# First cross attention: keys' projection and the last key's product in strips of 32 columns

## The chip, the cores and the metric

The kernel runs on one core of a Trainium2 chip. The metric is device time in microseconds; three runs of the kernel before took 3436.03 to 3438.41 us, with a median of 3437.31. All arithmetic around the change is in FP32. TensorE runs an FP32 matmul as two passes: every matmul of the code stands in the trace as two MATMULs and two LDWEIGHTS.

## What is computed

Six blocks act on `x` (128 x 32 x 256): a cross attention, a differential attention and a feed-forward block, then another three of the kind. The change touches the first block alone, which is, cut to what matters:

```python
x = x + xattn(layernorm(x), ctx)          # ctx: 128 batches x 257 keys x 256
q = rms_norm(linear(xn, q_w, q_b))        # 16 heads of 16
k = rms_norm(linear(ctx, k_img_w, k_img_b))
v = linear(ctx, v_img_w, v_img_b)
out = linear(softmax(q @ k.T * scale) @ v, o_w, o_b)
```

## The kernel before

The first cross attention (`image_attention`) goes through 128 slots, one per batch, in a software pipeline; four slots are one chunk of 128 tokens. `every_slot` writes out the first and the last slots and runs those between in a loop (`Fori`, line 137) whose body holds four. Each engine has its own program, in the order in which the code stands, and the engines wait for one another by semaphores. 257 keys are 256, which go through TensorE in two halves of 128, and a last one, whose terms are worked out apart.

TensorE's slot, function `tensor`, in this order:

- L366, the keys' projection for the batch two slots on: the context, transposed, is the weights (128 rows, 128 columns), `w_k` streams with 256 columns. Two halves of the keys times two of the contraction are 4 matmuls, 8 passes. Its end raises `k_full`, for which VectorE's L698 (`k_raw`) waits. It writes the PSUM bank `a_ps`.
- L376, four transposes of the scaled keys of the next batch. It waits for `turn_read[1]` of ScalarE and `k_scaled` of GpSimd.
- L381, the values' projection of the next batch, in the same form as L366. Its end raises `v_full`, behind which SyncE issues the load of a later context.
- an item of the chunk, one in each of four slots: output projection (L390), a transpose (L394), the queries (L398), a transpose (L405).
- L414 and L418, four transposes each, of this batch's weights of attention.
- L429, the scores of the next batch, as tiles of 32 rows and 64 columns.
- L442, the weighing: attention's weights times values, as 16 matmuls with 32 columns of weights each (tiles of 128 rows and 32 columns), the four in a row going to the four groups of 32 PSUM partitions of `out_ps`.
- L448, in every fourth slot: the last key's product for the chunk, two matmuls of 128 columns, into the other half of the same bank (`item_ps`). It waits for `v_last_ready` of GpSimd and for `p_rows_ready`, which VectorE raises at L746.

Then follows L366 of the next slot. The wait ahead of L366 is for `turn_read[0]` and for the context's load. In the trace, `128*32` in a row is the tile of the array: rows, columns. The second cross attention (`adapter_attention`) has a similar slot, with L976 for the scores (tiles of 32 rows and 128 columns), L980 for transposes and L1091 for the weighing (tiles of 128 rows and 32 columns).

Of the kernel before, what the change touches and what calls it, by code (L numbers as in the profile page):

```python
# [14 lines left out]
P = 128  # L15
D = 256
# [70 lines left out]
def ge(eng, sem, count):  # L87

    if not isinstance(count, int) or count > 0:
        eng.wait_ge(sem, count)  # L90
# [91 lines left out]
def image_attention(nc, io, stack):  # L182
# [16 lines left out]
    def sb(name, shape, dt=F32):  # L199
        return stack.enter_context(nc.sbuf_tensor(f"{name}_i", shape, dt))  # L200

    def pb(name):
        return stack.enter_context(nc.psum_tensor(f"{name}_i", [P, 512], F32))
# [9 lines left out]
    w_q, w_k, w_v, w_o = (sb(n, [P, 2, D]) for n in ("w_q", "w_k", "w_v", "w_o"))  # L213
# [7 lines left out]
    ctx_t = [sb(f"ctx_t{j}", [P, 2, 2 * P]) for j in range(4)]  # L221
# [8 lines left out]
    v_last_all, v_last_raw, v_last = sb("v_last_all", [P, D]), sb("v_last_raw", [P, D]), sb("v_last", [P, D])  # L230
# [6 lines left out]
    p_last, p_last_t, p_rows = sb("p_last", [P, L]), sb("p_last_t", [P, L]), sb("p_rows", [P, 4, L])  # L237
# [6 lines left out]
    q, q2, qn = sb("q", [P, D]), sb("q2", [P, D]), sb("qn", [P, D])  # L244
# [4 lines left out]
    a_ps, b_ps, c_ps, out_ps = pb("a_ps"), pb("b_ps"), pb("c_ps"), pb("out_ps")  # L249
    out_heads = out_ps[:, 0:P].rearrange("p (f h q) -> p f h q", f=2, h=2)  # L250
    item_ps, nf_sum_ps = out_ps[:, 2 * P:4 * P], out_ps[:, P:P + 3]
# [39 lines left out]
    def item_out(at):  # L291

        b = at.b()
        if b == 0:
            return y_ready, at.chunks(-1)
        return (None, xn_t_ready, q_raw, q_t_ready)[b], at.chunks(1)

    def has_item(at):
        return at.live_chunk(-1) if at.b() == 0 else at.live_chunk(1)
# [56 lines left out]
    def tensor(pe, before, ahead):  # L356
        def slot(at):
            if at.live(2):
                if at.live(-1):
                    pe.wait_ge(turn_read[0], at.count(-1))  # L360
                else:
                    ge(pe, k_raw_ready, at.count(1))
                pe.wait_ge(ctx_in[at.b(2)], at.chunk(2) * 16 + 16)
                for r in range(2):
                    for c in range(2):
                        last = pe.matmul(a_ps[:, r * D:r * D + D], ctx_t[at.b(2)][:, c, r * P:r * P + P], w_k[:, c, :], start=c == 0, stop=c == 1)  # L366
                last.then_inc(k_full, 1)
            if at.live(1):
                if at.live(-1):
                    pe.wait_ge(turn_read[1], at.count(-1))  # L370
                else:
                    ge(pe, k_ready, at.count(0))
                pe.wait_ge(k_scaled, at.count(1, 2))
                for f in range(2):
                    for r in range(2):
                        last = pe.transpose(b_ps[:, f * D + r * P:f * D + r * P + P], k_raw[at.b(1) % 2][:, r, f * P:f * P + P], ident)  # L376
                last.then_inc(k_turned, 1)
                ge(pe, v_ready, at.count(0))
                for r in range(2):
                    for c in range(2):  # L380
                        last = pe.matmul(c_ps[:, r * D:r * D + D], ctx_t[at.b(1)][:, c, r * P:r * P + P], w_v[:, c, :], start=c == 0, stop=c == 1)  # L381
                last.then_inc(v_full, 1)
            if has_item(at):
                if at.live(-1):
                    pe.wait_ge(out_read, at.count(-1))
                elif has_item(At(at.i, at.o - 1)):
                    ge(pe, *item_out(At(at.i, at.o - 1)))
                if at.b() == 0:
                    for f in range(2):
                        last = pe.matmul(item_ps, attn_t[:, f, :], w_o[:, f, :], start=f == 0, stop=f == 1)  # L390
                elif at.b() == 1:
                    pe.wait_ge(xn_ready, at.chunks(1))
                    for c in range(2):
                        last = pe.transpose(item_ps[:, c * P:c * P + P], xn[:, c * P:c * P + P], ident)  # L394
                elif at.b() == 2:
                    pe.wait_ge(xn_t_ready, at.chunks(1))
                    for c in range(2):
                        last = pe.matmul(item_ps, xn_t[:, c, :], w_q[:, c, :], start=c == 0, stop=c == 1)  # L398
                    if isinstance(at.i, int) and at.n() == NF_SUM:
                        pe.wait_ge(nf_total_ready, 1)  # L400
                        last = pe.matmul(nf_sum_ps[0:S, :], nf_ones[:, :], nf_total[:, :], start=True, stop=True)
                else:
                    pe.wait_ge(qn_ready, at.chunks(1))
                    for c in range(2):
                        last = pe.transpose(item_ps[:, c * P:c * P + P], qn[:, c * P:c * P + P], ident)  # L405
                last.then_inc(item_full[at.b()], 1)
            if isinstance(at.i, int) and at.n() == B - 1:
                for _ in range(8):
                    pe.matmul(b_ps[:, 0:D], w_k[:, 0, 0:P], w_k[:, 1, :], start=True, stop=True)
            if at.live():  # L410
                ge(pe, k_raw_ready, at.count(2))
                pe.wait_ge(probs_ready, at.count(0, T))
                for i in range(T):
                    last = pe.transpose(a_ps[:, i * P:i * P + P], probs[:, i, 0:P], ident)  # L414
                last.then_inc(turned[0], 1)
                ge(pe, k_ready, at.count(1))
                for i in range(T):
                    last = pe.transpose(b_ps[:, i * P:i * P + P], probs[:, i, P:2 * P], ident)  # L418
                last.then_inc(turned[1], 1)
            if at.live(1):  # L420
                pe.wait_ge(k_ready, at.count(1))
                pe.wait_ge(k_last_ready, at.count(1))
                pe.wait_ge(q_bd_ready, at.count(1))
                if not at.live():
                    pe.wait_ge(first_out, 3)
                for f in range(2):
                    for i in range(T):
                        rows = slice(32 * i, 32 * i + 32)
                        last = pe.matmul(s_ps[i][64 * f:64 * f + 64, 0:K], q_bd[at.b(1) % 2][rows, f, :, :].rearrange("p h q -> p (h q)"), k_n[rows, f, :], start=True, stop=True)  # L429
                        if f == 1:  # L430
                            last.then_inc(scores_done, 1)
            if at.live():
                if has_item(at):
                    ge(pe, *item_out(at))
                else:
                    ge(pe, out_read, at.count(-1))
                ge(pe, v_ready, at.count(0))
                for r in range(2):
                    pe.wait_ge(turn_read[r], at.count(0))
                    for f in range(2):  # L440
                        for g in range(4):
                            last = pe.matmul(out_ps[32 * g:32 * g + 32, f * 64:f * 64 + 64], v[at.b() % 2][:, r, f * P + 32 * g:f * P + 32 * g + 32],  # L442
                                             probs_t[r][:, g * P + f * 64:g * P + f * 64 + 64], start=r == 0 and f == 0, stop=r == 1, skip_group_check=True)
                if at.b() == 3:
                    pe.wait_ge(v_last_ready, at.chunks(0))
                    pe.wait_ge(p_rows_ready, at.chunks(0))
                    for f in range(2):
                        last = pe.matmul(item_ps[:, f * P:f * P + P], v_last[:, f * P:f * P + P], p_rows[:, :, :].rearrange("p b q -> p (b q)"),  # L448
                                         start=False, stop=True, skip_group_check=True)
                last.then_inc(out_done, 1)  # L450

        pe.wait_ge(const_ready, 1)
# [3 lines left out]
        for f in range(2):  # L456
            for c in range(2):
                last = pe.matmul(s_ps[0][:, f * P:f * P + P], w_k[:, c, f * P:f * P + P], ctx_last[:, c, :], start=c == 0, stop=c == 1)
        last.then_inc(first_full, 1)
        pe.wait_ge(const_in, 16)  # L460
        slot(At(-1, 0))
        slot(At(-1, 1))
        pe.wait_ge(first_ss_ms, 1)
# [3 lines left out]
        for c in range(2):  # L467
            last = pe.matmul(s_ps[2][:, 0:D], ctx_last[:, c, :], w_v[:, c, :], start=c == 0, stop=c == 1)
# [4 lines left out]
        for f in range(2):  # L473
            last = pe.matmul(s_ps[3][:, 0:D], v_b[:, f:f + 1].broadcast_to([P, P]), w_o[:, f, :], start=f == 0, stop=f == 1)
# [2331 lines left out]
```

## Time and profile before

| | |
|---|---|
| median of three runs | 3437.31 us |
| profiled execution | 3437.49 us, span 3435.6 us |
| first cross attention | about 12 to 916 us |
| PE, DVE, ACT, POOL busy in the span | 98%, 71%, 57%, 48% |
| PE busy between 12 and 916 us | 890 of 904 us |

PE is TensorE's matmul, PEld its loading of weights, DVE VectorE, ACT ScalarE, POOL GpSimd, SP SyncE. Passes of TensorE overlap, and their ends are modelled: the time that one pass takes of the engine is the distance from its start to the next one's start. A row of the timeline merges passes of one line; its first column is the start of the first, its second the distance from there to the end of the last.

### The profile page before, as it was taken

The numbers are of one execution on the slowest core, as the hardware profiler recorded it, in microseconds if no ns is written. First come the engines' busy times: TensorE is split into PE (matmuls) and PEld (weight loads), VectorE is DVE, ScalarE is ACT, GpSimd is POOL, SyncE is SP. The second block draws the span as 40 slices with busy tenths as digits, with TensorE's granted clock in tenths as the row PEclk, the third lists the DMA queues.
The fourth block names the chain that finished last, engine by engine and source line by source line (L and its number), as shares of the span: only waits on it lengthen the run. The fifth ranks groups of instructions, "written<-read, shape, count | busy, mean of one in ns | idle before, by whom it ended". The sixth has DMA issues, their size and how long they took to land.

```text
span 3435.6 us, 92591 instructions
## 1 busy us (share of the span) xinstructions
PE 3361.4 (98%) x29689; PEld 2484.9 (72%) x29698; DVE 2446.6 (71%) x7409; ACT 1960.2 (57%) x5935; POOL 1647.2 (48%) x3197
## 2 busy tenths in 40 slices
PE   9999999999899999999999999999999999999999
PEld 7888888888666767777777777777766666665555
DVE  5677877777787648888888888888868844444443
ACT  5777777777566537777776777776765411111111
POOL 4666666666565536655665565566546400000000
PEclk9999999999999999999999999999999999999999
DMA  3111111111212231111111111111135620000000
GB/s 96 57 54 53 56 53 53 55 53 56 65 51 70 81 109 44 45 46 42 44 46 42 48 46 41 45 46 42 47 79 145 184 64 20 20 19 20 19 19 9
DMA packets 280323, 187.59 MB, mean 55 GB/s; under 512 B 117165, under 2 KB 277125, under 8 KB 280213
## 3 DMA queue, kind: packets, MB, share of 16 engines
q1 hardware_dynamic: 279925, 185.75, 19.0%
q8 instruction: 66, 1.08, 0.1%
q10 hardware_dynamic: 288, 0.40, 0.1%
q14 instruction: 44, 0.36, 0.0%
HBM read 145.61 MB, written 36.21 MB: 53 GB/s over the span
## 4 chain that ended last, share of the span: by engine, by line
PE 51%; DVE 7%; issue 2%; ACT 2%; DMA 1%; SPq 0%; DVEq 0%; ACTq 0%; POOL 0%; POOLq 0%
PE bank_e L2551 13%; PE bank_e L2528 6%; PE a_ps_a L1011 5%; PE b_ps_a L969 5%; PE s_ps_a L976 4%; PE a_ps_a L980 3%; PE out_ps_a L1091 3%; PE c_ps_a L980 2%; PE b_ps_a L1023 2%; DVE neg_max_a L1203 2%; ACT probs_a L1112 1%; PE out_ps_a L1078 1%; PE m_ps_r L2146 1%; PE b_ps_a L1018 1%; PE b_ps_a L1036 1%
## 5 line engine op out<-in xcount | busy, mean ns | idle before, releaser
L1112 ACT ACTIVATE probs_a<-s_ps_a,neg_max_a 128x257 f32<-128x257 f32 x1024 | 472.2, 476 | 283.5 <-DVE neg_max_a L1203 283.5
L1154 POOL TENSOR_SCALAR probs_a<-probs_a,gated_a 128x256 f32<-128x256 f32 x1024 | 495.2, 503 | 269.3 <-DVE gated_a L1211 269.3
L1203 DVE TENSOR_REDUCE neg_max_a<-s_ps_a 128x1 f32<-128x257 f32 x1024 | 360.9, 414 | 0.0
L2577 ACT ACTIVATE gate_e<-bank_e 128x512 f32<-128x512 f32 x128 | 76.4, 597 | 493.1 <-PE bank_e L2551 493.0
L523 POOL TENSOR_SCALAR probs_i<-probs_i,inv_sum_i 128x256 f32<-128x256 f32 x512 | 244.8, 492 | 127.9 <-DVE inv_sum_i L687 123.4
L2694 DVE TENSOR_TENSOR hidden_e<-gate_e,bank_e 128x512 f32<-128x512 f32 x128 | 87.3, 687 | 292.5 <-PE bank_e L2551 290.9
L2509 POOL TENSOR_TENSOR inv_std_e<-var_eps_e,half_e 128x4 f32<-128x4 f32 x8 | 8.1, 1010 | 567.2 <-DVE var_eps_e L2591 567.2
L507 ACT ACTIVATE probs_i<-s_ps_i,neg_max_i 128x257 f32<-128x257 f32 x512 | 236.3, 474 | 69.7 <-DVE neg_max_i L758 68.0
L366 PE MATMUL a_ps_i<-w_k_i,ctx_t_i 128*128 128x256 f32 x1024 | 253.6, 391 | 5.5 <-issue 5.5
L1011 PE MATMUL a_ps_a<-w_v_a,ctx_t_a 128*128 128x256 f32 x1024 | 256.7, 394 | 0.0
L381 PE MATMUL c_ps_i<-w_v_i,ctx_t_i 128*128 128x256 f32 x1024 | 242.2, 379 | 0.0
L2551 PE MATMUL bank_e<-xn_t_e,w_gate_e 128*128 128x512 f32 x512 | 241.3, 593 | 0.0
L969 PE MATMUL b_ps_a<-ctx_t_a,w_qk_a 128*128 128x256 f32 x1016 | 240.4, 379 | 0.4 <-issue 0.4
L2551 PE MATMUL bank_e<-xn_t_e,w_up_e 128*128 128x512 f32 x512 | 240.6, 592 | 0.0
L1011 PEld LDWEIGHTS a_ps_a<-w_v_a,ctx_t_a 128*128 128x128 f32 x1024 | 184.8, 190 | 69.8 <-issue 25.5
L2528 PEld LDWEIGHTS bank_e<-w_down_e,hidden_e 128*128 128x128 f32 x1024 | 194.6, 190 | 50.3 <-issue 26.8
L2528 PE MATMUL bank_e<-w_down_e,hidden_e 128*128 128x256 f32 x1024 | 230.1, 379 | 0.0
L366 PEld LDWEIGHTS a_ps_i<-w_k_i,ctx_t_i 128*128 128x128 f32 x1024 | 185.4, 191 | 36.7 <-issue 10.4
L758 DVE TENSOR_REDUCE neg_max_i<-s_ps_i 128x1 f32<-128x257 f32 x512 | 181.3, 415 | 41.2 <-PE s_ps_i L429 41.1
L1112 ACT ACTIVATION_READ_ACCUMULATOR probs_a<-s_ps_a,neg_max_a 128x1 f32 x1024 | 210.4, 205 | 0.0
L976 PE MATMUL s_ps_a<-k_t_a,q_bd_a 32*128 32x289 f32 x2048 | 197.0, 454 | 11.9 <-ACT probs_a L1112 6.7
L381 PEld LDWEIGHTS c_ps_i<-w_v_i,ctx_t_i 128*128 128x128 f32 x1024 | 184.6, 190 | 19.8
(365 smaller groups left out, 8059.7 us busy)
## 6 DMA issues: line engine op xcount, KB each, us to landing
ctx_t_i<-in_ctx_t SPq DMA_DIRECT2D x128, 256.0 KB, 2.7
ctx_t_a<-in_ctx_t SPq DMA_DIRECT2D x128, 256.0 KB, 2.7
mask_a<-in_L_xattn_mask SPq DMA_DIRECT2D x512, 4.0 KB, 1.5
v_bd_a<-v_self_a SPq DMA_DIRECT2D x512, 8.0 KB, 1.8
x_tok_i<-in_x SPq DMA_DIRECT2D x32, 128.0 KB, 2.0
x_res_i<-in_x SPq DMA_DIRECT2D x32, 128.0 KB, 2.4
x_after<-y_tok_i SPq DMA_DIRECT2D x32, 128.0 KB, 1.7
x_tok_d<-x_after SPq DMA_DIRECT2D x32, 128.0 KB, 2.2
```

The costliest lines, as they stand in the source:

```text
L366: last = pe.matmul(a_ps[:, r * D:r * D + D], ctx_t[at.b(2)][:, c, r * P:r * P + P], w_k[:, c, :], start=c == 0, stop=c == 1)
L381: last = pe.matmul(c_ps[:, r * D:r * D + D], ctx_t[at.b(1)][:, c, r * P:r * P + P], w_v[:, c, :], start=c == 0, stop=c == 1)
L507: act.activation(probs[:, i, :], s_ps[i][:, 0:K], ACT.Exp, bias=neg_max[:, i:i + 1], accum_out=row_sum[:, i:i + 1]).then_inc(exp_done, 1)
L523: pool.tensor_scalar(probs[:, i, 0:2 * P], probs[:, i, 0:2 * P], inv_sum[:, i:i + 1], 1.0, ALU.mult, ALU.mult).then_inc(probs_ready, 1)
L969: last = pe.matmul(into[:, f * n:f * n + n], w_qk[:, c, D + f * P:D + f * P + P], ctx[:, c, 0:n], start=c == 0, stop=c == 1)
L976: pe.matmul(s_ps[:, g, 0:N], q_bd[j][rows, f, :, :].rearrange("p h q -> p (h q)"), k_t[j][rows, f, :], start=True, stop=True).then_inc(sco ...
L1011: last = pe.matmul(a_ps[:, r * D:r * D + D], ctx_t[at.b(1)][:, c, r * P:r * P + P], w_v[:, c, :], start=c == 0, stop=c == 1)
L1112: act.activation(probs[:, t, :], s_ps[:, g, 0:K], ACT.Exp, bias=neg_max[:, t:t + 1], accum_out=row_sum[:, t:t + 1]).then_inc(exp_done, 1)
L1154: pool.tensor_scalar(probs[:, t, 0:2 * P], probs[:, t, 0:2 * P], gated[:, t:t + 1], 1.0, ALU.mult, ALU.mult).then_inc(probs_ready, 1)
L1203: dve.tensor_reduce(neg_max[:, 4 * f + g:4 * f + g + 1], s_ps[:, g, 0:K], AX.X, ALU.max, negate=True).then_inc(max_ready, 1)
L2528: last = pe.matmul(w[:, t * D:t * D + D], hidden[e % 2][:, k, tok:tok + P], w_down[:, e, k, :], start=k == 0, stop=k == TILES - 1)
L2551: last = pe.matmul(w[:, :], weights[:, e, c, t * P:t * P + P], xn_t[:, c, :], start=c == 0, stop=c == 1)
```

## The change

The four matmuls of L366 become sixteen: each takes 32 columns of the context as weights and writes 32 PSUM partitions. The two of L448 become eight in the same way. Operands, sums, waits, semaphores and the order of the lines stay as they are.

```diff
-                        last = pe.matmul(a_ps[:, r * D:r * D + D], ctx_t[at.b(2)][:, c, r * P:r * P + P], w_k[:, c, :], start=c == 0, stop=c == 1)
+                        for g in range(4):
+                            last = pe.matmul(a_ps[32 * g:32 * g + 32, r * D:r * D + D], ctx_t[at.b(2)][:, c, r * P + 32 * g:r * P + 32 * g + 32], w_k[:, c, :],
+                                             start=c == 0, stop=c == 1, skip_group_check=True)
...
-                        last = pe.matmul(item_ps[:, f * P:f * P + P], v_last[:, f * P:f * P + P], p_rows[:, :, :].rearrange("p b q -> p (b q)"),
-                                         start=False, stop=True, skip_group_check=True)
+                        for g in range(4):
+                            last = pe.matmul(item_ps[32 * g:32 * g + 32, f * P:f * P + P], v_last[:, f * P + 32 * g:f * P + 32 * g + 32], p_rows[:, :, :].rearrange("p b q -> p (b q)"),
+                                             start=False, stop=True, skip_group_check=True)
```

## Rows read from the trace of the kernel before

**Rows 1.** The page: busy time, chain that ended last, shortest DMA to land.

```profile
PE 3361.4 (98%) x29689; PEld 2484.9 (72%) x29698; DVE 2446.6 (71%) x7409; ACT 1960.2 (57%) x5935; POOL 1647.2 (48%) x3197
...
PE 51%; DVE 7%; issue 2%; ACT 2%; DMA 1%; SPq 0%; DVEq 0%; ACTq 0%; POOL 0%; POOLq 0%
...
mask_a<-in_L_xattn_mask SPq DMA_DIRECT2D x512, 4.0 KB, 1.5
```

**Rows 2.** Busy time by stretch: us, each engine, granted clock, DMA share, GB/s.

```profile
12.00:916.00 904.00, 890.14 (x10264) 726.57 (x10264) 677.09 (x2108) 661.96 (x2143) 579.39 (x1153) 1.00 0.19 57
```

**Rows 3.** TensorE's waits, 12 to 916 us: total us, times, longest us.

```profile
PE a_ps_i L366 <- issue: 5.5, 29, 0.2
...
PE b_ps_i L376 <- POOL k_raw_i L543: 1.1, 1, 1.1
```

**Rows 4.** Timeline of TensorE: start us, us, instruction.

```profile
407.37 0.65 PE L442 MATMUL out_ps_i<-probs_t_i,v_i 128*32 128x64 f32 x32
...
410.22 1.89 PE L381 MATMUL c_ps_i<-w_v_i,ctx_t_i 128*128 128x256 f32 x8
```

**Rows 5.** Timeline of TensorE around L366 in an ordinary slot, partly in narrow windows.

```profile
407.80 0.22 PE L442 MATMUL out_ps_i<-probs_t_i,v_i 128*32 128x64 f32 x1
...
407.95 1.99 PE L366 MATMUL a_ps_i<-w_k_i,ctx_t_i 128*128 128x256 f32 x8
...
408.27 0.38 PE L366 MATMUL a_ps_i<-w_k_i,ctx_t_i 128*128 128x256 f32 x1
...
409.78 0.60 PE L376 MATMUL b_ps_i<-const_i,k_raw_i 128*128 128x128 f32 x4
```

**Rows 6.** Timeline of TensorE in the second cross attention, partly in narrow windows.

```profile
1503.37 0.42 PE L976 MATMUL s_ps_a<-k_t_a,q_bd_a 32*128 32x289 f32 x4
1503.72 0.33 PE L980 MATMUL a_ps_a<-const_a,probs_a 128*128 128x128 f32 x1
...
1503.88 0.38 PE L980 MATMUL a_ps_a<-const_a,probs_a 128*128 128x128 f32 x2
...
1507.35 1.08 PE L1091 MATMUL out_ps_a<-probs_t_a,v_a 128*32 128x128 f32 x32
```

**Rows 7.** Timeline of TensorE behind the loop's branch, partly in narrow windows.

```profile
421.87 0.22 PE L442 MATMUL out_ps_i<-probs_t_i,v_i 128*32 128x64 f32 x1
...
422.29 1.99 PE L366 MATMUL a_ps_i<-w_k_i,ctx_t_i 128*128 128x256 f32 x8 [0.20 <-issue]
424.11 0.60 PE L376 MATMUL b_ps_i<-const_i,k_raw_i 128*128 128x128 f32 x4
```

**Rows 8.** Line 137, 100 to 850 us: ns min/median/max, first and last start.

```profile
L137 PEldq COMPARE_BRANCH  x27: 215/215/220, 115.9 to 838.6; - x27
```

**Rows 9.** Busy time by stretch: one pass of either cross attention's loop.

```profile
394.16:421.95 27.79, 27.48 (x328) 22.52 (x320) 22.17 (x68) 20.69 (x67) 18.25 (x37) 1.00 0.18 54
1378.22:1417.94 39.72, 39.45 (x375) 30.70 (x370) 34.44 (x112) 28.11 (x92) 23.77 (x54) 1.00 0.17 45
```

**Rows 10.** Timeline of TensorE and VectorE around L448, partly in narrow windows.

```profile
414.13 0.29 DVE L746 TENSOR_TENSOR p_rows_i<-p_last_t_i,const_i 128x128 f32<-128x128 f32 x1
...
414.31 0.24 PE L442 MATMUL out_ps_i<-probs_t_i,v_i 128*32 128x64 f32 x4
414.57 0.68 PE L448 MATMUL out_ps_i<-p_rows_i,v_last_i 128*128 128x128 f32 x4
...
416.82 0.38 PE L376 MATMUL b_ps_i<-const_i,k_raw_i 128*128 128x128 f32 x2
```

**Rows 11.** Line 448: idle time of its engine before it, us and times.

```profile
  issue: 3.5, 22
```

**Rows 12.** The same as group 10 in a later slot.

```profile
691.43 0.29 DVE L746 TENSOR_TENSOR p_rows_i<-p_last_t_i,const_i 128x128 f32<-128x128 f32 x1
...
692.40 0.23 PE L442 MATMUL out_ps_i<-probs_t_i,v_i 128*32 128x64 f32 x2
...
694.84 0.27 PE L376 MATMUL b_ps_i<-const_i,k_raw_i 128*128 128x128 f32 x1
```

## Prediction

> **What bounds the kernel now.** I read the page first, for the share of each engine, then the busy time by stage, the waits of TensorE in the stage that the diff touches, the timeline of a few of its slots, and last narrow windows of that timeline, since the question is one of tenths of a microsecond. The page has TensorE busy for 98% of the span and on half of the chain that ended last [rows 1]. The first cross attention is the stretch from 12 to 916 us: TensorE is busy for 890 of 904 us there, at a granted clock of 1.00, which is the 2.4 GHz level [rows 2]. In the whole stretch it waits for another engine's work for some 8 us, and the only wait of its own that comes back regularly is 29 times 0.2 us at L366 [rows 3]. So this stage lasts as long as TensorE's own stream, and all that lies between the starts of its passes counts: what the diff saves or adds there moves the end by as much. "Busy" hides such losses, because the modelled end of a pass lies behind the start of the next one; starts have to be compared.
>
> **What a change of tiling costs.** A pass of 256 columns through the whole array starts 0.216 us behind the one before it (8 passes of L381 in 1.89 us, the last alone 0.38, so 7 steps in 1.51) [rows 4]. The weighing (L442) runs in strips: its 32 passes in four column groups take 0.65 us, 0.22 of them the last pass alone, so 0.43 between first and last start: 7 steps from one group of four to the next of 0.056 us, 0.02 for the four starts within a group, and 0.02 more once, for the first, short weight loads [rows 4]. Now the boundary to the keys' projection (L366): the last strip starts at 407.80, the projection at 407.95, its second pass only at 408.27 [rows 5]. Without a change of tiling the next pass would start 0.056 - 0.02 = 0.04 us behind the last strip. It starts 0.15 behind it, which is 0.11 lost; the second pass comes 0.32 instead of 0.216 later, since the first weights were not loaded ahead: 0.10 lost. From the last strip to the first turn of keys (L376, 409.78) it is 1.98 us. Between the projection and L376 nothing is lost (the last pass starts 0.38 before the end of the group at 409.94, so at 409.57, and L376 0.216 later) [rows 5], since both use the whole array.
>
> **What the change does: it moves that boundary, it does not remove it.** The projection becomes 16 matmuls with 32 columns of weights instead of 4 with 128, so 32 passes instead of 8, in 8 groups of four; multiplications, bytes and waits are the same. The turns behind it (L376) still use the whole array, and so the tiling changes between L366 and L376 now. No row shows strips followed by L376. The nearest ones are in the second cross attention: behind the 32-row strips of L976 (289 columns, 0.24 us of streaming at the rate above) the transpose L980 starts 0.33 us after the last strip (1503.39 to 1503.72), and its second pass 0.16 later instead of 0.11 [rows 6]. So a drain of 0.09 behind the end of the stream and 0.055 for the uncovered weights [rows 6], which is half of the 0.10 at L366. That half is all that the change has to win.
>
> That four strips of a projection run side by side at full speed is the second thing without a row. The nearest is L1091, strips of the same shape with 128 columns: 32 passes in 1.08 us less 0.27 for the last, 0.81 = 7 x 0.109 + 0.02 + 0.025, and 0.109 is the step of whole-array passes of 128 columns too (four of L376 from 409.78 to L381 at 410.22) [rows 4 to 6]. I take 0.216 for 256 columns. Its bounds: nothing lost, or the first group's 0.025 lost again in each group.
>
> **The Trainium skill**, in TensorEngine Tiling, Key Properties, says that changing the tiling mode drains the engine, not merely changing the tile. The 0.15 at L442 to L366 agrees [rows 5]; by that rule the count of changes decides, and it stays three in a slot. The same page, under Restrictions, says that column tiling rules out the FP32 transpose mode; no run here shows it. By that the turns could not follow in strips, and the drain has to come back in front of them.
>
> **The sum, by kind of slot,** each from the last strip of the weighing to L376.
> Ordinary (62 slots, two in four): 1.98 now. After: 0.04, then 7 x 0.216 = 1.51 to the last group, 0.02 to its last strip, 0.213 of streaming and 0.096 of drain, and 0.055 of uncovered weights: 1.935. Minus 0.045 each, -2.8 us.
> Behind the loop's branch (29 slots, those of L366's waits [rows 3]): TensorE's sequencer branches for 0.215 us [rows 8], and the projection starts 0.42 us behind the last strip (421.87 to 422.29), with L376 at 424.11: 2.24 us [rows 7]. The drain in front of L366 costs nothing here, as it lies under the branch. After: 0.42 + 0.025 + 1.51 + 0.02 + 0.31 + 0.055 = 2.34. Plus 0.10 each, +2.8 us.
> Slots with the last key's product (31, one in four). In 23 of them, up to 667 us, L448 waits for `p_rows` (22 such waits are long enough to be listed [rows 11]): VectorE ends it at 414.42, L448 starts at 414.57, the last strip had started at 414.33; L376 follows at 416.82, 2.49 us [rows 10]. The wait covers the drain here too, and it stays: `p_rows` hangs on VectorE's order behind L405 of this same slot, and from L405 to L442 nothing changes. After: 0.24, 0.025 and 4 groups x 0.109 for L448, then 1.51 + 0.02 + 0.31 + 0.055 = 2.60. Plus 0.11 each, +2.5 us. In the other 8, once VectorE has left the quantizer's steps behind, `p_rows` is ready long before (691.72): 2.43 now (692.41 to 694.84) [rows 12], after 0.04 + 0.44 + 1.895 = 2.375; -0.4 us.
> The first two projections have no strips ahead of them, so they pay a change of tiling on both sides: +0.3 us.
> Together +2.4 us: the half of a weight load that is won in two slots of four is lost where a branch or a wait had been covering the drain.
>
> Two terms with a bound. TensorE's sequencer must have issued the strips in time: it issues the 64 instructions of the weighing between two of its own steps, in under 0.6 us, and stands just a few loads ahead at the boundary. If it comes late by up to 0.05 us there, 70 slots cost up to 3.5 us more; I take 0, as L442 itself keeps a step of 0.056 per four strips, a quarter of the 0.216 that is needed here [rows 4]. If the transposes' weights should be loaded during the drain, 124 x 0.055 = 6.8 us less; I take 0.055, by L980. `k_full` comes 0.2 us earlier against the turns in ordinary slots; VectorE's L698 needs it, but no wait of TensorE hangs on it. L376 waits for `k_scaled` of POOL, and only once for 1.1 us; coming 0.1 earlier, it finds it ready [rows 3]. SP's loads of the context are issued behind `v_full`, which moves by 0.1 us at most and lies three slots ahead of its use.
>
> The profiled execution took 3437.49 us for a span of 3435.6; the median of the runs is 3437.31, so they are alike, and I predict 3437.31 + 2.4 = 3439.7 us.
>
> **The rivals.**
> The change does not do what it says: the drain in front of L366 stays, because what drains is not the tiling but any change of shape. Then the ordinary slots pay both sides, 62 x 0.13 = 8 us more, some 3448. Against it: L366 to L376 changes line, operands and columns without loss as long as the tiling is the same [rows 5]. Chance 4%.
> The whole boundary goes: the turns behind strips start without drain or load. Ordinary slots then win 1.98 - 1.77 = 0.21 (13 us), slots behind the branch and with a wait 0.07 (3.6 us), the other 8 0.23 (1.8 us): 3419. For it speaks that the stretch from L442 to L366 is now one stream. Against it is L980 behind L976 [rows 6]. Chance 6%. A half-way case, the drain stays but the load is hidden, gives 3437.31 + 2.4 - 6.8 = 3433. Chance 12%.
> Slower: strips of 256 columns do not keep the pace of 0.216, because four weight loads and four streams of moving columns, all reading the same `w_k`, come at once. There are 128 x 8 = 1024 groups, so from 0.007 us per group on (3%) it is a measurable loss; with the 0.025 of a first group in every one of the other seven it is 22 us, 3462. For it: no strip with more than 128 columns is in the trace. Against it: L1091 is exact at 128. Chance 9%.
> Slower as well: the loop's body on TensorE grows from 648 instructions by 4 x 48 + 24 to 864, above the 745 of the second cross attention [rows 9]. Were the branch to wait for instructions from memory, at no less than the 1.5 us in which the shortest transfer lands [rows 1], 27 to 29 passes of the loop would add 43 us: 3483. For it: no body so large is in the trace. Against it: the branches of the loop that is there take 0.215 us, with the wait behind them as short as 0.2 [rows 8, 3]. Chance 4%. The Trainium skill (Runtime: NRT & Kernel Launch, Instruction fetch mechanics) gives TensorE room for 2048 instructions; by that page nothing is fetched again.
>
> **How the numbers follow.** The forecast itself, with its bounds, has 65%: from 3433 (load hidden) to 3443.5 (sequencer late), and a microsecond for the spread of the medians. With the half-way case it is 77%; the range 3431.5 to 3445.0 takes in these and a small part of the slower rivals. A measurement of this kernel can tell 0.2%, 6.9 us, from no change: faster is below 3430.4, slower above 3444.2. Faster 0.08, same 0.76, slower 0.16.
>
> **What the profile of the changed kernel will show.** L366 as 4096 passes of 128*32, first one 0.04 us behind the last strip of L442 in ordinary slots, 0.42 behind a branch; its groups of four 0.216 apart, L376 0.31 behind the last strip and its second pass 0.16 later. L448 as 512 passes, still starting 0.24 behind L442 up to 667 us. Slots of one kind as long as before within 0.1 us. I am wrong if the groups are further apart, if the branch takes more than 0.22, or if L376 starts less than 0.3 behind the last strip.

## The result, and the profile after

The changed kernel takes 3441.07 us (median of 20 runs, 3435.96 to 3445.16), the kernel before 3435.11 (20 runs, 3433.04 to 3438.41): a ratio of 1.0016, 95% interval 1.0009 to 1.0022. That is some 6 us more, and less than the 0.2% taken as the bound of "no change". The profiled execution has a span of 3438.9 us, 3.3 more than before.

The first cross attention first. Timeline of TensorE in the changed kernel (start us, us, instruction), partly in narrow windows; L444 is the weighing, L367 the keys' projection, L378 the turns of the keys, L383 the values' projection, L451 the last key's product:

```profile
406.50 0.65 PE L444 MATMUL out_ps_i<-probs_t_i,v_i 128*32 128x64 f32 x32
406.97 1.91 PE L367 MATMUL a_ps_i<-w_k_i,ctx_t_i 128*32 128x256 f32 x32
408.81 0.66 PE L378 MATMUL b_ps_i<-const_i,k_raw_i 128*128 128x128 f32 x4
409.30 1.89 PE L383 MATMUL c_ps_i<-w_v_i,ctx_t_i 128*128 128x256 f32 x8
...
408.50 0.38 PE L367 MATMUL a_ps_i<-w_k_i,ctx_t_i 128*32 128x256 f32 x1
...
413.40 0.22 PE L444 MATMUL out_ps_i<-probs_t_i,v_i 128*32 128x64 f32 x1
...
413.65 0.65 PE L451 MATMUL out_ps_i<-p_rows_i,v_last_i 128*32 128x128 f32 x16
414.08 1.94 PE L367 MATMUL a_ps_i<-w_k_i,ctx_t_i 128*32 128x256 f32 x32
415.95 0.33 PE L378 MATMUL b_ps_i<-const_i,k_raw_i 128*128 128x128 f32 x1
...
421.04 0.24 PE L444 MATMUL out_ps_i<-probs_t_i,v_i 128*32 128x64 f32 x4
421.47 1.93 PE L367 MATMUL a_ps_i<-w_k_i,ctx_t_i 128*32 128x256 f32 x32 [0.19 <-issue]
423.34 0.66 PE L378 MATMUL b_ps_i<-const_i,k_raw_i 128*128 128x128 f32 x4
```

Against [rows 5]: the last strip of the weighing starts at 406.93 (406.50 + 0.65 - 0.22), the first of the projection 0.04 later instead of 0.15, and then nothing is lost within the projection: last strip at 408.50, so 7 x 0.216 + 0.02 behind the first. The turns start 0.31 behind that last strip, and the values' projection follows 0.49 us behind the turns' start instead of 0.44 (0.055 of uncovered weights). In all 1.88 us from strip to turns, 1.93 with the weights, against 1.98 in this slot; over the 65 ordinary slots it is 0.041 us less on average. Against [rows 10]: L451 starts 0.25 behind the last strip, as before; the turns 2.55 behind it instead of 2.49, plus 0.055. Against [rows 7]: 0.41 and 2.28, plus 0.055, instead of 0.42 and 2.24. Over all slots that is, from the first to the last pass of the values' projection (start of the first, start of the last, on the right):

```profile
L381 PE MATMUL c_ps_i<-w_v_i,ctx_t_i x1024: 379/379/382, 22.1 to 905.6; 128*128 128x256 f32 x171
```

in the kernel before, 883.5 us, and in the changed one

```profile
L383 PE MATMUL c_ps_i<-w_v_i,ctx_t_i x1024: 379/379/382, 19.8 to 905.2; 128*128 128x256 f32 x171
```

885.4 us: **1.9 us more**, where 2.4 was forecast. (The changed kernel came to its first pass 2.3 us earlier: the granted clock between 11 and 18 us was 1.00 in that execution and 0.51 in the one before. That is outside the change, and a second execution of it began at 21.8. Between the first and the last pass of the values' projection the clock was at its upper level throughout, in every profile of this study.)

**The other loss is far from the change**, in the fifth block (self attention of the second three), from its first transposes to the first transposes of the sixth. Kernel before, then after:

```profile
2554.60 1.09 PE L2133 MATMUL m_ps_r<-const_r,xn_r 128*128 128x128 f32 x8
2746.76 1.35 PE L2536 MATMUL bank_e<-ident_e,xn_e 128*128 128x128 f32 x8
```

```profile
2554.20 1.09 PE L2136 MATMUL m_ps_r<-const_r,xn_r 128*128 128x128 f32 x8
2749.89 1.35 PE L2539 MATMUL bank_e<-ident_e,xn_e 128*128 128x128 f32 x8
```

192.2 us against 195.7: **3.5 us more** in a block whose code is the same. In the stretch between the two cross attentions (last pass of the values' projection to the first of L969, at 1273.74 us and 1273.32) the kernels take 368.2 and 368.1 us, from there to the fifth block both take 1280.9, and behind the fifth block 688.8 and 689.0. In the fifth block, what first meets the eye is a wait for transfers. TensorE's waits between 2550 and 2760 us, before and after:

```profile
PE s_ps_r L2154 <- DMA by_dim_q_r<-scratch_q: 2.4, 3, 1.5
```

```profile
PE s_ps_r L2157 <- DMA by_dim_q_r<-scratch_q: 6.2, 6, 2.1
```

These two lines alone prove little. The kernel before has another 3.3 us at the same line, put down to ScalarE, and TensorE is idle for 17.4 us of the block before and 17.6 after. It is busy for 3.3 us more after (178.1 against 174.7), and its clock was at the lower level for 13.7 us of the block instead of 6.8. So the clock is a rival; it is taken up behind the experiments.

The block writes keys and queries to memory and reads them back in another order; SyncE issues the reading once the writing has landed. One such pair in the fourth turn, before and after, by the times of issue (the writing, then the reading):

```profile
2629.45 0.56 SPq L2036 DMA_DIRECT2D scratch_q<-proj_t_q_r  x1
2633.64 1.34 SPq L2041 DMA_DIRECT2D by_dim_q_r<-scratch_q  x2
```

```profile
2629.60 0.61 SPq L2039 DMA_DIRECT2D scratch_q<-proj_t_q_r  x1
2635.03 1.34 SPq L2044 DMA_DIRECT2D by_dim_q_r<-scratch_q  x2
```

And DMA between the issue of the writing and that of the reading (queues with packets, MB and share; then the issue with its time to landing).

```profile
q1 hardware_dynamic: 2254, 0.76, 93.4%
issues: line engine op xcount, KB each, median us to landing
scratch_q<-proj_t_q_r SPq DMA_DIRECT2D x1, 256.0 KB, 4.2
```

```profile
q1 hardware_dynamic: 2222, 0.75, 68.1%
q8 instruction: 1, 0.02, 1.4%
issues: line engine op xcount, KB each, median us to landing
scratch_q<-proj_t_q_r SPq DMA_DIRECT2D x1, 256.0 KB, 5.4
```

```profile
q8 instruction: 66, 1.08, 0.1%
```

```profile
q8 instruction: 69, 1.13, 0.1%
```

and the growth of TensorE's program fits the three: a written-out projection has 48 more instructions and there are 12 of them (8 outside the loop, 4 in it), a last key's product 24 more in 3 places: 648 instructions, 2.5 packets of 256. Hence a theory for the fifth block: it is written out, its instructions are streamed in while it runs (20 packets of queue 8 in the kernel before), and by the change each packet is fetched at another point of a turn, the 648 leaving a remainder of 136 when divided by the 256 that a packet holds. The rival was that strips, or the clock, or chance made the difference. The experiments bear on both parts, the first cross attention and the fifth block.

### The profile page after: what moved, and what is told of

Read it like the earlier page. It is cut to its first block, busy times and chain, and to the rows that moved or that the text cites. A ratio compares the mean times of both kernels' runs of the same rounds, so it can differ in the third digit from the quotient of the medians.

```text
span 3438.9 us, 99512 instructions
## 1 busy us (share of the span) xinstructions
PE 3365.5 (98%) x33154; PEld 2413.9 (70%) x33154; DVE 2448.5 (71%) x7409; ACT 1960.4 (57%) x5935; POOL 1648.4 (48%) x3197
## 4 chain that ended last, share of the span: by engine, by line
PE 50%; DVE 7%; DMA 2%; issue 2%; ACT 1%; SPq 0%; DVEq 0%; ACTq 0%; POOL 0%; POOLq 0%
PE bank_e L2554 13%; PE bank_e L2531 6%; PE a_ps_a L1014 5%; PE b_ps_a L972 5%; PE s_ps_a L979 4%; PE a_ps_a L983 3%; PE out_ps_a L1094 3%; PE c_ps_a L983 2%; PE b_ps_a L1026 2%; DVE neg_max_a L1206 2%; ACT probs_a L1115 1%; PE out_ps_a L1081 1%; PE m_ps_r L2149 1%; DMA scratch_q<-proj_t_q_r 1%; DMA by_dim_q_r<-scratch_q 1%
## 5 line engine op out<-in xcount | busy, mean ns | idle before, releaser
L367 PE MATMUL a_ps_i<-w_k_i,ctx_t_i 128*32 128x256 f32 x4096 | 246.0, 380 | 5.2 <-issue 5.2
L383 PE MATMUL c_ps_i<-w_v_i,ctx_t_i 128*128 128x256 f32 x1024 | 242.2, 379 | 0.0
L972 PE MATMUL b_ps_a<-ctx_t_a,w_qk_a 128*128 128x256 f32 x1016 | 240.4, 379 | 0.4 <-issue 0.4
L383 PEld LDWEIGHTS c_ps_i<-w_v_i,ctx_t_i 128*128 128x128 f32 x1024 | 184.6, 190 | 19.8
L972 PEld LDWEIGHTS b_ps_a<-ctx_t_a,w_qk_a 128*128 128x128 f32 x1016 | 183.1, 190 | 20.5 <-DVE v_self_a L1252 0.9
```

The lines of the kernel that those rows point to most:

```text
L367: last = pe.matmul(a_ps[32 * g:32 * g + 32, r * D:r * D + D], ctx_t[at.b(2)][:, c, r * P + 32 * g:r * P + 32 * g + 32], w_k[:, c, :], star ...
L972: last = pe.matmul(into[:, f * n:f * n + n], w_qk[:, c, D + f * P:D + f * P + P], ctx[:, c, 0:n], start=c == 0, stop=c == 1)
```

## The experiments

All lengths in one table, each from one profiled execution: A is the first cross attention (first to last pass of the values' projection), B the fifth block, "place" the instructions added to TensorE ahead of the fifth block, modulo 256. "Low clock" is the time within B for which TensorE's clock was granted at its lower level, "delayed" how many of the block's eight writings of queries were delayed, which is explained behind the experiments.

| kernel | place | A, us | B, us | low clock, us | delayed | ratio to before, 95% interval |
|---|---|---|---|---|---|---|
| before | 0 | 883.5 | 192.2 | 6.8 | 0 | |
| before again | 0 | 883.5 | 192.6 | 10.2 | 0 | 0.9999 (0.9990 to 1.0008) |
| changed | 136 | 885.4 | 195.7 | 13.7 | 4 | 1.0016 (1.0009 to 1.0022) |
| changed again | 136 | 885.5 | 196.0 | 13.7 | 4 | 1.0018 (1.0009 to 1.0027) |
| strips in L366 alone | 64 | 891.8 | 199.1 | 10.2 | 4 | 1.0037 (1.0025 to 1.0049) |
| strips in L448 alone | 72 | 886.7 | 196.9 | 13.7 | 3 | 1.0027 (1.0017 to 1.0038) |
| before, 136 instructions more | 136 | 883.4 | 195.9 | 10.2 | 4 | 1.0007 (0.9998 to 1.0016) |
| changed, 120 more | 0 | 885.6 | 192.1 | 13.7 | 0 | 1.0011 (1.0002 to 1.0020) |
| before, 72 more | 72 | 883.2 | 196.8 | 10.2 | 5 | 1.0018 (1.0009 to 1.0028) |
| strips in two slots of four, 224 more | 0 | 880.0 | 192.3 | 10.2 | 0 | 0.9991 (0.9982 to 1.0000) |
| the same again | 0 | 880.1 | 194.1 | 13.7 | 0 | 0.9994 (0.9985 to 1.0003) |
| two slots, none more | 32 | 885.7 | 198.4 | 20.5 | 5 | 1.0019 (1.0010 to 1.0028) |
| two slots, 164 more | 196 | 879.9 | 197.1 | 13.7 | 3 | 1.0002 (0.9993 to 1.0011) |
| before, 96 more | 96 | 888.6 | 198.3 | 13.7 | 2 | 1.0025 (1.0016 to 1.0034) |

**Both kernels a second time.**

> The kernel before, unchanged, as a second profile of it. Both theories: ratio 1.000 within 0.0005; the first cross attention (first to last pass of the values' projection) 883.4 us as before, within 0.2. Theory A (what the change costs is the moved boundary alone, about 2 us in the first cross attention; the further 3.5 us in the fifth block of the one profile of after are the luck of its DMAs and of the clock): the fifth block (first pass of the transposes of its normalized input to the first pass of the next block) may take anything between 192 and 196 us here as well. Theory B (the change also lengthens the fifth block, for instance by the larger program): it takes 192 us here, within 0.5.

> The changed kernel, unchanged, as a second profile of it. First cross attention 1.9 us longer than before by both theories. Theory A: fifth block anywhere between 192 and 196 us, ratio between 1.0005 and 1.0015. Theory B: fifth block 195 us or more again, ratio 1.0012 to 1.0022.

B came out at 192.6 and 196.0, the ratio of the changed kernel at 1.0018. That is what theory B said. Theory A had allowed both lengths and missed only the ratio (1.0015 at most), so two executions of each kernel make chance unlikely and do not rule it out; the kernels with padding, below, decide it.

**Keys' projection alone, last key's product alone.** Each takes one of the two edits of the diff and leaves the other line as it was.

```diff
 # e3: L366 as in the change; L448 stays
-                        last = pe.matmul(a_ps[:, r * D:r * D + D], ...)
+                        for g in range(4):
+                            last = pe.matmul(a_ps[32 * g:32 * g + 32, r * D:r * D + D], ...)
 # e4: L448 as in the change; L366 stays
-                        last = pe.matmul(item_ps[:, f * P:f * P + P], ...)
+                        for g in range(4):
+                            last = pe.matmul(item_ps[32 * g:32 * g + 32, f * P:f * P + P], ...)
```

> Only the keys' projection in strips, the last key's product whole. Boundary theory: in every fourth slot the tiling now changes three times around the last key's product (weighing to L448, L448 to L366, L366 to L376), so those 31 slots grow by 0.28 us each instead of 0.11: first cross attention +9 us against before (31 x 0.28 = 8.7, +2.8 behind the branch, -2.8 in the ordinary slots, +0.3 at the start), time +0.26%. Rival (the loss comes from strips of 256 columns being slow, not from boundaries): as with the whole change or less, +2 us or under in the stage, since it has fewer strips.

> Only the last key's product in strips, the keys' projection whole. Boundary theory: L448 starts no earlier in the 23 slots in which it waits for p_rows, and the drain, formerly covered by that wait, then stands behind it: +0.15 us in each of the 23, 0 in the 8 others: +3.6 us in the first cross attention, +0.1%. Rival (strips pay by themselves as they avoid a change of tiling): a gain, -0.1 us in each of 31 slots, -3 us.

A grew by 8.3 us with the projection alone (9 expected) and by 3.2 with the last product alone (3.6 expected); the rival had a gain for the second and 2 us for the first. Timeline of TensorE around the last key's product, projection alone:

```profile
416.87 0.65 PE L444 MATMUL out_ps_i<-probs_t_i,v_i 128*32 128x64 f32 x32
417.55 0.68 PE L450 MATMUL out_ps_i<-p_rows_i,v_last_i 128*128 128x128 f32 x4
418.16 1.93 PE L367 MATMUL a_ps_i<-w_k_i,ctx_t_i 128*32 128x256 f32 x32
420.03 0.66 PE L378 MATMUL b_ps_i<-const_i,k_raw_i 128*128 128x128 f32 x4
```

and last product alone:

```profile
415.02 0.65 PE L442 MATMUL out_ps_i<-probs_t_i,v_i 128*32 128x64 f32 x32
415.71 0.64 PE L449 MATMUL out_ps_i<-p_rows_i,v_last_i 128*32 128x128 f32 x16
416.28 1.99 PE L366 MATMUL a_ps_i<-w_k_i,ctx_t_i 128*128 128x256 f32 x8
418.11 0.60 PE L376 MATMUL b_ps_i<-const_i,k_raw_i 128*128 128x128 f32 x4
```

The last strip of the weighing lies at 417.30 and 415.45. From it to the turns: 2.73 us (three changes of tiling) and 2.66 (one, but behind the wait for `p_rows`, which covered it before), against 2.49 before. In each, the product starts 0.25 behind the strip, whatever its tiling: what could be won there is under the wait. Each change of tiling that nothing covers costs what the model says.

**The place of the packets, without any strips, and strips without the displacement.** TensorE's program is lengthened in its idle time ahead of the first weights; the number of small matmuls sets the length (four instructions each; here 3 for the long ones left out and 34 for the 136 instructions):

```diff
-        for _ in range(10):
+        for _ in range(7):
             pe.matmul(s_ps[3][:, 0:D], v_last_raw[:, 0:P], v_last_raw[:, :], start=True, stop=True)
+        for n in range(37):
+            g = n % 4
+            pe.matmul(s_ps[3][32 * g:32 * g + 32, 0:L], v_last_raw[:, 32 * g:32 * g + 32], v_last_raw[:, 0:L], ...)
```

> The kernel before with 136 more instructions for TensorE (34 more warm-up matmuls of 32x32 in the idle time ahead of the first weights, three of the long warm-up ones left out for them). 136 is what the change adds to TensorE's program (648 = 12 written-out projections x 48 + 3 last-key products x 24) modulo 256, the instructions of one 16 KB packet of its instruction queue. Packet theory (the fifth block is written out, its instructions are streamed in, and what counts is where in a turn the 16 KB packets fall among the transfers): first cross attention as before within 0.2 us, fifth block 195 to 196.5 us as in both profiles of after, against 192.2 and 192.6; time +3 to +4 us, +0.1%. Rival (it is the strips or the later start of the block): fifth block 192 to 193 us, ratio 1.000.

> The changed kernel with 120 more instructions for TensorE at its start in the same way, so that it has 768 = 3 x 256 more than the kernel before and its packets fall as in the kernel before. Packet theory: first cross attention +1.9 us, fifth block back to 192 to 193 us, time +2 us against before, ratio 1.0006. Rival: fifth block 195.7 to 196, ratio 1.0017 as without the padding.

> The kernel before with 72 more instructions for TensorE at its start, which is what strips for the last key's product alone add. Packet theory: first cross attention as before, fifth block 196 to 198 us as in that kernel (196.9), time +4 to +5 us; nearly the phase of the kernel with the keys' projection alone (576 = 2 x 256 + 64), whose block took 199.1. Rival: fifth block 192 to 193.

Fifth block of the three, its first transposes and those of the sixth: before with 136 more,

```profile
2551.17 1.09 PE L2136 MATMUL m_ps_r<-const_r,xn_r 128*128 128x128 f32 x8
2747.08 1.35 PE L2539 MATMUL bank_e<-ident_e,xn_e 128*128 128x128 f32 x8
```

changed with 120 more,

```profile
2553.98 1.09 PE L2139 MATMUL m_ps_r<-const_r,xn_r 128*128 128x128 f32 x8
2746.03 1.41 PE L2542 MATMUL bank_e<-ident_e,xn_e 128*128 128x128 f32 x8
```

and before with 72 more:

```profile
2551.47 1.09 PE L2136 MATMUL m_ps_r<-const_r,xn_r 128*128 128x128 f32 x8
2748.29 1.35 PE L2539 MATMUL bank_e<-ident_e,xn_e 128*128 128x128 f32 x8
```

195.9, 192.1 and 196.8: a kernel without strips has the block of the changed one, the changed one gets its old block back, and 72 instructions give the block of the kernel with which they share the place (196.9). The rival would have left 192, 196 and 192. The whole times fit less well than the block: 136 more cost 2.6 us where 3 to 4 was expected, and 120 more brought the changed kernel from 1.0016 and 1.0018 to 1.0011, where 1.0006 was expected; the intervals of 0.0009 either way allow both. 72 more cost 5.9 us where 4 to 5 was expected. Other stretches differ between the profiles too: in "before, 136 more", 1266.4 us lie between a projection at the head of the second cross attention (L972, at 1284.73 us; L969, at 1286.45, in the kernel before) and the fifth block, instead of 1268.2. That need not be the place: in the last 4.6 us ahead of the fifth block the granted clock was 0.63 in the kernel before, and 1.00 in the padded one. The two were not separated.

**The clock as a rival for the fifth block.** The profiles settle it. With the clock low for the same 10.2 us, B takes 192.6 and 192.3 us at place 0 and 195.9, 196.8 and 199.1 at places 136, 72 and 64; with 13.7 us it takes 192.1 and 194.1 at place 0 and 195.7 to 198.3 elsewhere. The place moves the block at an equal clock. What lies behind the 2 us between the two at place 0 is not known.

**What a packet does, in all profiles.** The block writes queries eight times, so the fourteen profiles hold 112 such writings. From the issue of the writing's second half to that of the reading it takes 4.00 to 4.44 us in the 41 in which no packet of queue 8 was under way, and 3.97 to 4.54 us in the 37 in which one started 3.0 us or more behind the issue. In the other 34 a packet started between 0.4 us ahead of the issue and 2.9 us behind it, and there it takes 4.69 to 5.92 us: these are the delayed ones of the table. At place 0 every packet that meets a writing comes late in it, and none is delayed; at place 136 four of eight are, in each of three profiles. A turn (from one such writing to the next) that has the upper clock throughout lasts 21.4 us on average without a delayed writing (59 turns) and 22.5 with one (22 turns). These are delays found together with packets; only the place was set by experiment. They do not make up the whole of B: "before, 96 more" has only two delayed writings and yet 198.3 us, its other turns taking 22.0 to 22.8 us, and the 194.1 of place 0 has none.

**Strips only where they win.** In two slots of four, those with neither the branch nor the last product ahead of them, the projection is in strips; elsewhere all is as before.

```diff
+                        if at.b() in (2, 3):
+                            for g in range(4):
+                                last = pe.matmul(a_ps[32 * g:32 * g + 32, r * D:r * D + D], ...)
+                        else:
                             last = pe.matmul(a_ps[:, r * D:r * D + D], ...)
```

> The kernel before with the keys' projection in strips only in the two ordinary slots of four (those behind neither the loop's branch nor the last key's product), the last key's product whole, and 224 more instructions at the start (288 + 224 = 512 = 2 x 256). Boundary theory: only the slots that win 0.045 us are left, first cross attention -2.8 us; with the packets as before the fifth block 192 to 193; time -2.8 us, -0.08%: faster than both kernels, though hardly to be told by the time alone. Rival (a change of tiling costs the same wherever it stands): first cross attention unchanged within 0.3 us.

> The two-slot kernel with its packets placed as before, a second time: first cross attention 3.5 us shorter, fifth block 192.3, ratio 0.999 again (both theories).

> Strips for the keys' projection in the two ordinary slots of four alone, without padding: 288 more instructions for TensorE, 32 past a full packet. Boundary theory: first cross attention 3 us shorter, as with the padding (3.47 measured there). Packet theory: the fifth block is not 192.2 (that is the place of the packets in the kernel before) but what this place gives, which only the run can tell; between 190 and 199 by the places seen so far. Rival (the padding at the start and not the place of the packets moves the fifth block): 192.2.

> The same with 164 more instructions at the start: 452, 196 past a full packet, a place not yet seen. First cross attention 3 to 3.5 us shorter; fifth block between 190 and 199 us. If it is under 192.2, this kernel is the fastest of all.

With the packets where they were, A is 3.5 and 3.4 us shorter: 3.0 from the 65 ordinary slots (0.046 each, where the model had 0.045 in 62) and 0.4 from the slots behind the branch, whose wait shrank by 0.015 us each. The times were 1.5 and 1.1 us below the kernel before, ratios 0.9991 and 0.9994: the lowest of the study, but neither interval leaves out 1, and B was 194.1 the second time where 192.3 was expected, so the place fixes the block to 2 us and no better. With 164 more (place 196) A keeps its gain at 879.9, B is 197.1, and the whole stands at 1.0002. Without padding (place 32) it is slower than the kernel before, 1.0019: B is 198.4, and A lost its gain as well, which I had not expected. That loss is in the waits behind the loop's branch. TensorE's waits between 100 and 850 us, two slots with no padding:

```profile
PE a_ps_i L371 <- issue: 9.5, 27, 0.5
```

against 5.0 us in the same 27 of the kernel before. The last run asked whether that hangs on the two forms in one loop or on where the loop begins in its packet; the unpadded kernel has 96 instructions more ahead of the loop.

> The kernel before with 96 more instructions for TensorE at its start, no strips anywhere. 96 is what the unpadded two-slot kernel has ahead of the first cross attention's loop (two written-out projections x 48); there the waits of the projection behind the loop's branch came to 9.5 us in 27 instead of 5.0. Place theory: where the loop begins within a 16 KB packet sets the wait behind its branch, so these waits are 9 to 10 us again and the first cross attention is 4.5 to 5.5 us longer than before, with no change to its matmuls; the fifth block has its packets at a place not yet seen, 192 to 199. Rival (the two kinds of projection in one loop body make the wait): waits 5.0 us, first cross attention as before.

```profile
PE a_ps_i L366 <- issue: 9.6, 27, 0.5
```

No strips, the same waits, A longer by 5.1 us: two forms in one loop are not needed for it, the displacement is enough. Not every displacement does it: the kernels with 72 and 136 more have 4.8 and 5.0 us there. Why a loop that begins 96 instructions further on waits longer is not known. The eleven times of this kernel reach from 3436.9 to 3448.0 us and the profiled one, 3447.8, is the second longest, so the waits may not be as long in each of them.

## Why the prediction was right or wrong

**The time** was forecast as 3439.7 with a range of 3431.5 to 3445.0 and lies at 3441.07; the forecast move was +2.4 us, the measured one about 6 (ratio 1.0009 to 1.0022, 3 to 7.6 us). "Same" was right by the bound of 0.2%. So the verdict came out, but by the profiles more than half of the move (3.5 of 5.4 us) has a cause that the prediction did not have. That 3439.7 lies within 1.4 us of the measured time is luck: the forecast started from 3437.31, the median of three runs, where twenty give 3435.11, and this 2.2 us made up for part of what the move lacked.

**The boundary moves and does not go**: right, step by step. The first strip of the projection 0.04 behind the weighing, groups 0.216 apart, turns 0.31 behind the last strip, 0.055 of uncovered weights: all as worked out. Means over the slots of each kind: the 65 ordinary ones -0.04 us (forecast -0.045 in 62), the 29 behind the branch +0.08 (+0.10; the wait itself shrank by 0.01), the 23 with the wait for `p_rows` +0.11 (+0.11), the other eight -0.06 (-0.055). That sums to the 1.9 measured, against 2.4: the slots behind the branch account for 0.4 of the difference, and the 0.3 taken for the first two projections is not tested, since A begins behind the first of them and the clock differs there. The two partial kernels, where the same terms give other sums, confirm the model with 8.3 for 9 and 3.2 for 3.6.

**The two bounds that were left open**: strips of 256 columns do keep the pace, and the sequencer comes in time; the transposes' weights are not loaded during the drain (0.055, as L980 had it).

**The step that failed** is the rival of the larger program, and with it the term for everything outside the first cross attention, which was put at nothing. It asked only whether the loop's branch would wait for instructions from memory, found that it does not, which the changed kernel confirms (branch 0.21 us, waits behind it 5.2 us in 29 against 5.5 in [rows 3]), and ended there with "by that page nothing is fetched again". Right of the loops: queue 8 brought no packet between 100 and 800 us, in either kernel. But behind it come stretches that are written out, the whole fifth block among them, and their instructions arrive as 16 KB packets, which the profile counts on the same 16 DMA engines as the data. The 648 instructions displaced every later packet, and the fifth block, which waits for its transfers, was 3.5 us longer: more than the change itself cost.

**Of the Trainium skill**, TensorEngine Tiling (Key Properties) said that a change of mode drains the engine; with 0.09 to 0.10 us at each uncovered boundary, plus the weights, the runs agree. Runtime: NRT & Kernel Launch (Instruction fetch mechanics) says that instructions come in blocks of 16 KB, of 256 instructions each, and that crossing a boundary is mostly hidden. The size agrees with the places found here: programs with the same remainder by 256 gave the same block to 0.6 us, except for one profile in five at place 0 (194.1 against 192.1 to 192.6). That the crossing is hidden does not hold in a block that waits for its transfers, where the measured 3.5 to 6.9 us decide. The prediction took from the same section only that TensorE has room for 2048 instructions. The section also says that a taken branch to a target outside the current window of two pages has to wait for a fetch, and two blocks of 256 are 512 instructions; the loops here, of 648 and 864 instructions, show no such fetch. So "nothing is fetched again" is what the traces show, but the section can be read either way.

## What to carry to other kernels

Before putting work into the tiling of its neighbour, count the changes of tiling around the whole slot, with a drain and an uncovered weight load at each: moving one is worth something only if its new place is one that a wait or a branch covers, and costs if the old place was (what remained here in the ordinary slots is the 0.04 us between two weight loads). When a few microseconds in a partly written-out program are at stake, give both kernels the same length in instructions modulo a packet, or compare block by block; a ratio of the whole would have ascribed to the strips 3.5 us that belong to the place of unrelated instruction packets.

## What the runs showed of the hardware

A drain at a change of tiling is 0.09 to 0.10 us behind the end of the last stream, in each direction and for streams of 64 to 289 columns (with streaming taken at 0.213 us for 256 columns, the next pass starts 0.150 us behind the start of one of 64, 0.309 behind one of 256 and 0.332 behind one of 289), and a transpose behind it lacks 0.055 us of weights where a matmul lacks 0.10. The place of instruction packets moved a block of 192 us that waits for transfers in every turn by up to 6.9 us (places 0, 32, 64, 72, 96, 136, 196: 192.2, 198.4, 199.1, 196.9, 198.3, 195.7, 197.1; profiles at place 0 differed by up to 2.0). One packet that started up to 2.9 us behind the issue of a writing of 256 KB made the time to the next issue 4.69 to 5.92 us instead of 3.97 to 4.54; one that started at 3.0 us or later did not. A program displaced by 96 instructions had waits behind its loop's branch of 0.36 us a time instead of 0.19 (9.6 and 5.0 us in 27); displaced by 72 or 136 it did not. That a packet shares a DMA engine with the delayed piece of the transfer is argued from the emptying queues (in the fourth turn they are nearly empty for the last microsecond), not shown.
